# FFN 1's output bias and half of a dot-product sum on GpSimd, and another order of the work on four engines

## The chip, the cores and the metric

The kernel runs on one core of a Trainium2 chip. Five engines run their own instruction streams and meet only at semaphores: TensorE (matmuls into PSUM), VectorE, ScalarE, GpSimd, and SyncE, which here only issues DMAs. The metric is the device time of one execution in microseconds.

## The reference, cut to what matters

The input is 16 images of 96 channels and 96 x 96 pixels; the output has the same shape. Two layers follow each other, each a convolution-like part and a quantized feed-forward network (FFN), with residual sums.

- Layer 0's convolution cuts an image into 3 x 3 patches. In each patch all 9 pixels are scored against 512 vectors (cosine similarity). The best pixel and its best vector are mixed into 96 numbers; with the 9 similarities of that vector they pass a small MLP (leaky ReLU, tanh, ReLU), a linear layer and a 1 x 1 convolution, which gives the patch's 3 x 3 x 96 outputs.
- Each FFN takes a normalized pixel x (96 numbers) and computes `q(W2 q(relu(q(W1 q(x)) + b1))) + b2` with inputs and weights rounded to a float with 2 mantissa bits and sums rounded to 16 bits; the hidden layer has 384 units.
- Layer 1's convolution is a local response normalization (LRN): each pixel is divided by a power of 2 + 1e-4 times a 5 x 5 box sum of squared norms.

## The kernel before, in words

A tile is 128 patches (1152 pixels), and there are 128 tiles, 8 per image. One body is written out for each of 145 steps; each step works on a different tile in each stage, so that all engines always have work. `PARTS` gives the tile of each stage by its offset from the step: `fs` (load, token statistics) is 4 ahead, `f1` (pixel scores) 3, `f2` (window's best vector) 2, `f3` (MLP and conv) 1, `back` (FFN 0's hidden layer) 0, `tail` (its output) -1, `pre`/`rear`/`rtail` (LRN normalization, FFN 1's hidden layer, its output) -11 to -13. The order in which each engine takes the stages' pieces is written out by hand in `body` of that engine; nothing is reordered later, so an instruction that waits holds up all behind it on its engine.

The pieces that the change touches:

- TensorE: `scores(j0, j1)` (L415) are two matmuls per pixel j into one of two PSUM banks, freed by VectorE's maximum. `hidden_units` (L392) and `out_units` (L400) are the FFNs' first and second layer; each FFN has two banks, refilled when ScalarE has copied them. Units 0 to 8 are 3 chunks of 128 hidden units by 3 column groups of 512, 512 and 128; the output is two units of 5 and 4 pixels. `mlp_turn`, `mlp_in`, `mlp_mid`, `mlp_last`, `conv` (L433 to L460) are the MLP, each waiting for a ScalarE step; `win_turn` and `win_scores` (L422, L428) score the chosen pixel.
- ScalarE: `take_hidden` and `take_out` (L552) copy banks to SBUF as f16, `lrn_pixels` (L598) scales x2 into x3, `norm0` and `norm1` (L585) write the FFNs' inputs, `inpT`, `winT`, `h`, `vcs`, `h1` are the MLP's steps.
- VectorE: `score_max` (L824) takes the maximum over 512 scores of a bank. `relu` (L903) adds the bias and applies ReLU to a chunk of 1152 f16 numbers, `round_up` (L911) rounds all 3456 at once. `group_stats` (L815) are per-pixel statistics, `moments`, `pixel_roots` and `select` are chains of small instructions in which each waits for the one before (`run(chain, n)` issues n links), `win_vector` (L864) finds the window's vector. `mlp_input` sums `prod_dot` over channels (L874, 128 x 9 x 96 to 128 x 9), then three scalar products (L875 to L877, once a step), and forms the MLP's input. `residual1` (L894) adds the conv's result to x. `ffn_bias` (L920) adds the FFN's output bias, for FFN 1 and FFN 0 both on VectorE. `lrn_columns`, once an image, is a chain of some 30 links, dealt out between other pieces by `factors`.
- GpSimd: in this order per step, after `root_ready` (the last link of `pixel_roots`, L777): the residual add x2 of FFN 0 (L1080), the gather of the window's vector (an indirect DMA), `keep_root2` (a copy, L1094), `window_parts` once an image, the product `prod_dot` of token tile and vector (L1075), the residual add x4 of FFN 1 (L1080), `tile_columns` (a copy, L1087), the gather of the chosen pixel (L1059).
- SyncE's queue per step: FFN 0's transposes, the store of x4, the loads of the next token tile and of its channel form, FFN 1's transposes.

## Time and profile before

| | us |
|---|---|
| median of 3 runs | 3355.06 (3355.01 to 3362.01) |
| profiled execution, whole | 3366.41 |
| its span in the profile | 3364.6 |
| VectorE busy | 3022.2 (90%) |
| TensorE busy | 2824.8 (84%) |
| ScalarE busy | 2608.5 (78%) |
| GpSimd busy | 1192.6 (35%) |
| mean granted TensorE clock | 0.957 of full speed |

Busy times are shares of the profiled span; an engine's name in the rows is PE (TensorE), PEld (its weight loads), DVE (VectorE), ACT (ScalarE), POOL (GpSimd) or SPq (SyncE's queue). A number such as L911 is the line of the kernel that issued the instruction. The profile's chain of waits that ended last runs over VectorE for 36% of the span, ScalarE 26%, TensorE 25% and DMA 7%.

### The profile page before, as it was taken

What the parts mean: (1) busy time and instruction counts of PE and PEld (TensorE: products, weight loads), DVE (VectorE), ACT (ScalarE), POOL (GpSimd) and SP (SyncE); (2) the same over time, 40 slices, a digit from 0 to 9 for tenths busy, and PEclk for the clock granted to TensorE, in tenths of its full rate; (3) what the DMA queues carried; (4) which work ended last, traced back from release to release, by engine and by line L of the source; (5) the groups of instructions that cost most, each with busy time, mean ns of one, the idle gap of its engine ahead of it and who ended that gap; (6) DMA issues with size and microseconds to landing.
All of it is one profiled execution on the core that took longest, in us unless ns stands there. A gap on an engine that the chain in (4) does not pass through costs nothing.

```text
span 3364.6 us, 55888 instructions
## 1 busy us (share of the span) xinstructions
PE 2824.8 (84%) x15886; PEld 1512.2 (45%) x15886; DVE 3022.2 (90%) x10843; ACT 2608.5 (78%) x7047; POOL 1192.6 (35%) x1159
## 2 busy tenths in 40 slices
PE   5888898988888888888888888888989899889654
PEld 2444444444445444444444444444444445444322
DVE  6888999999999999999999999999999999999532
ACT  0444788888888887878888788888888888888876
POOL 1223243333334333333433433334343434334221
PEclk9999999999999999999999999999999999999755
DMA  3111222222222222232232222223222223232111
GB/s 91 48 55 47 66 69 84 80 72 81 71 73 80 69 83 66 69 82 67 68 84 65 73 79 68 84 68 83 71 82 71 83 70 84 68 84 58 37 48 43
DMA packets 236607, 237.32 MB, mean 71 GB/s; under 512 B 183426, under 2 KB 186764, under 8 KB 236300
## 3 DMA queue, kind: packets, MB, share of 16 engines
q1 hardware_dynamic: 226060, 214.86, 23.2%
q0 software_dynamic: 10240, 18.89, 2.2%
q8 instruction: 129, 2.11, 0.3%
q14 instruction: 178, 1.46, 0.1%
HBM read 134.72 MB, written 57.02 MB: 57 GB/s over the span
## 4 chain that ended last, share of the span: by engine, by line
DVE 36%; ACT 26%; PE 25%; DMA 7%; issue 5%; SPq 0%; POOL 0%; POOLq 0%; DVEq 0%
ACT ffn_hid L552 11%; ACT ffn_x L585 10%; PE banks L415 10%; DVE st L815 7%; DMA ffn_xT<-ffn_x 7%; DVE ffn_hid L911 7%; DVE pix L824 6%; DVE ffn_hid L903 6%; PE banks L392 4%; PE banks L460 4%; PE banks L400 3%; DVE x L894 3%; PE banks L438 2%; ACT h L665 2%; ACT x L598 1%
## 5 line engine op out<-in xcount | busy, mean ns | idle before, releaser
L552 ACT ACTIVATE ffn_hid<-banks 128x512 f16<-128x512 f32 (+1 forms) x2304 | 1052.7, 492 | 387.3 <-PE banks L392 386.6
L415 PE MATMUL banks<-wcT,xc 128*128 128x512 f32 x2304 | 1217.8, 620 | 79.7 <-DVE pix L824 43.6
L392 PE MATMUL banks<-ffn_xT,w1q 128*128 128x512 fp8e5 (+1 forms) x2304 | 706.7, 340 | 260.1 <-ACT ffn_hid L552 170.4
L1080 POOL TENSOR_TENSOR x<-x,ffn_f 128x864 f32<-128x864 f32 x256 | 491.7, 1921 | 1038.5 <-DVE nb L777 920.3
L824 DVE TENSOR_REDUCE pix<-banks 128x1 f32<-128x512 f32 x1152 | 787.1, 684 | 69.0 <-PE banks L415 68.7
L392 PEld LDWEIGHTS banks<-ffn_xT,w1q 128*128 128x128 bf16 x2304 | 219.5, 98 | 783.7 <-ACT ffn_hid L552 541.5
L400 PE MATMUL banks<-w2q,ffn_hid 128*128 128x96 bf16 x6912 | 394.6, 211 | 160.7 <-DVE ffn_hid L911 159.9
L903 DVE TENSOR_SCALAR ffn_hid<-ffn_hid,b1q 128x1152 f16<-128x1152 f16 x768 | 419.3, 559 | 116.0 <-ACT ffn_hid L552 116.0
L400 PEld LDWEIGHTS banks<-w2q,ffn_hid 128*128 128x128 f16 x6912 | 353.1, 101 | 364.1 <-issue 335.0
L598 ACT ACTIVATE x<-x,cols 128x96 f32<-128x96 f32 x1152 | 511.7, 473 | 0.0
L585 ACT ACTIVATE ffn_x<-x,cols 128x96 fp8e5<-128x96 f32 x1152 | 501.4, 485 | 0.0
L415 PEld LDWEIGHTS banks<-wcT,xc 128*128 128x128 f32 x2304 | 392.7, 194 | 209.5 <-DVE pix L824 69.1
L585 ACT ACTIVATE ffn_x<-x,nb,pix 128x96 fp8e5<-128x96 f32 x1152 | 481.2, 469 | 0.0
L815 DVE BATCH_NORM_STATS2 st<-x 128x6 f32<-128x96 f32 x2304 | 424.5, 244 | 19.4 <-POOL x L1080 19.4
L552 ACT ACTIVATE ffn_y<-banks 128x480 f16<-128x480 f32 (+1 forms) x512 | 274.7, 537 | 215.2 <-PE banks L400 215.1
L460 PE MATMUL banks<-wc,h 128*128 128x480 f32 (+1 forms) x1024 | 415.0, 550 | 2.3 <-ACT h L665 2.2
L1075 POOL TENSOR_TENSOR prod_dot<-xt,wrow 128x864 f32<-128x864 f32 x128 | 294.9, 2304 | 164.5 <-DMA wrow<-vector_table,vidx 164.5
L911 DVE TENSOR_SCALAR ffn_hid<-ffn_hid 128x3456 uint16<-128x3456 uint16 x256 | 318.3, 1243 | 4.9
L1059 POOL DMA_INDIRECT win<-x_tok_in,xrow x128 | 142.9, 1117 | 477.4 <-DVE xrow L844 477.4
L460 PEld LDWEIGHTS banks<-wc,h 128*128 128x128 f32 x1024 | 191.8, 195 | 246.4 <-issue 126.8
L1067 POOL DMA_INDIRECT wrow<-vector_table,vidx x128 | 127.0, 992 | 416.1 <-DVE vidx L864 407.7
L815 DVE BATCH_NORM_STATS2 st<-xt 128x6 f32<-128x96 f32 x1152 | 209.8, 244 | 4.8 <-DMA xt<-x_tok_in 4.8
(137 smaller groups left out, 2849.9 us busy)
## 6 DMA issues: line engine op xcount, KB each, us to landing
xt<-x_tok_in SPq DMA_DIRECT2D x128, 432.0 KB
xc<-x_chan_in SPq DMA_DIRECT2D x128, 432.0 KB
out_tok<-x SPq DMA_DIRECT2D x128, 432.0 KB
ffn_xT<-ffn_x SPq DMA_TRANSPOSE x256, 2.6
win<-x_tok_in,xrow POOLq DMA_INDIRECT x128, 3.1
wrow<-vector_table,vidx POOLq DMA_INDIRECT x128, 2.7
shift<-shift_in SPq DMA_DIRECT2D x1, 960.0 KB
vector_table<-wtab SPq DMA_DIRECT2D x1, 384.0 KB, 2.9
```

The source lines that it names most:

```text
L392: last = pe.matmul(bank[:, 0:c1 - c0], w1q[:, ffn.layer, c * P:(c + 1) * P], pairs, start=True, stop=True)
L400: last = pe.matmul(bank[:, (j - j0) * C:(j - j0 + 1) * C], ffn.hid[:, c, j * P:(j + 1) * P], w2q[:, ffn.layer, c, :], start=(c == 0), stop ...
L415: last = pe.matmul(ps_score[score_bank(j)], xc[p][:, j, :], wcT[:, :], start=True, stop=True)
L460: last = pe.matmul(bank[:, 0:(j1 - j0) * C], h1[:, q, :], wc[:, q, j0 * C:j1 * C], start=(q == 0), stop=(q == 1))
L552: return nc.scalar.activation(dst, src, ACT.Copy)
L585: last = nc.scalar.activation(ffn.x8[:, j // 2, 0:C, j % 2], x[:, j, :], ACT.Identity, bias=bias_c[:, j:j + 1], scale=scale_c[:, j:j + 1], ...
L598: last = nc.scalar.activation(x3[:, k.pre3, j, :], x2[:, k.pre & RING - 1][:, j, :], ACT.Identity, bias=cols[k.q][:, 1, j:j + 1], scale=co ...
L815: last = nc.vector.bn_stats(st3[:, which, j, :], src[:, j, :])
L824: nc.vector.tensor_reduce(mx[p][:, j:j + 1], ps_score[score_bank(j)], AX.X, ALU.max).then_inc(score_taken, 1)
L903: nc.vector.tensor_scalar(ffn.hid[:, c, :], ffn.hid[:, c, :], b1q[:, ffn.layer, c:c + 1], 0.0, ALU.add, ALU.max).then_inc(ffn.rounded, 1)
L911: nc.vector.tensor_scalar(bits, bits, TO_E5M2, TO_E5M2, ALU.add, ALU.subtract).then_inc(ffn.hid_ready, 1)
L1080: tt(dst, x, ffn.f[:, :, :], ALU.add).then_inc(ready, 1)
```

## The change

- FFN 1's bias (`ffn_bias(ffn1, ...)`) is taken from VectorE and done on GpSimd, between the gather and `window_parts`.
- After the product `prod_dot` (96 products per pixel) GpSimd adds its two halves into `half_dot` (48 per pixel), after the x4 add; VectorE's sum L874 then reads `half_dot`. A semaphore `dot_chain` orders the two.
- GpSimd's product also waits for `ffn1.hid_ready`, that is for VectorE's `round_up(ffn1)` of the same step.
- GpSimd's copies `keep_root2` and `tile_columns` move to the head of its step, except in the steps with `lrn_columns`, where they stay behind.
- VectorE's step begins with the maximum of score 0; the first three token statistics move into `mlp_input`, the other statistics are split into groups of three; five links of the root chain come in a row; FFN 0's bias comes after the root chain; `relu(ffn1, ...)`, the maxima and `select`/`moments` change places.
- TensorE issues scores 0 and 1 before FFN 0's output units, whose halves now have a score and a hidden unit of FFN 1 between them; the other pieces are moved as shown. ScalarE follows TensorE's order.

```diff
         prod_dot = sb("prod_dot", [P, J, C])
+        half_dot = sb("half_dot", [P, J, C // 2])
         dots = sb("dots", [P, J])
...
-        prod_dot_ready, inp_ready = sem("prod_dot_ready"), sem("inp_ready")
+        dot_chain, prod_dot_ready, inp_ready = sem("dot_pool_chain"), sem("prod_dot_ready"), sem("inp_ready")
...
@@ TensorE, body @@
-        scores(0, 1)
+        scores(0, 2)
         out_units(ffn0, k.tail, k.tail_p, 0)
-        scores(1, 2)
+        scores(2, 3)
+        hidden_units(ffn1, k.rear, 0, 1)
         out_units(ffn0, k.tail, k.tail_p, 1)
-        scores(2, 3)
+        hidden_units(ffn1, k.rear, 1, 2)
         if k.f3 is not None:
             mlp_turn(k.f3)
-        hidden_units(ffn1, k.rear, 0, 2)
+        hidden_units(ffn1, k.rear, 3, 1)
+        if k.f2 is not None:
+            win_turn(k.f2, k.q)
         if k.lrn is not None:
             pe.wait_ge(box_ready, k.lrn + 1)
         if k.f3 is not None:
             mlp_in(k.f3)
-        if k.f2 is not None:
-            win_turn(k.f2, k.q)
-        hidden_units(ffn1, k.rear, 2, 2)
+        hidden_units(ffn1, k.rear, 4, 1)
         scores(3, WIN_TURN)
-        hidden_units(ffn1, k.rear, 4, 1)
         if k.f3 is not None:
             if k.f2 is not None:
                 pe.wait_ge(winT_ready, k.f2 + 1)
             mlp_mid(k.f3)
-        hidden_units(ffn1, k.rear, 5, 2)
+        hidden_units(ffn1, k.rear, 5, 1)
         if k.f2 is not None:
             win_scores(k.f1, k.f2)
+        hidden_units(ffn1, k.rear, 6, 1)
+        scores(WIN_TURN, 5)
+        hidden_units(ffn1, k.rear, 7, 1)
+        scores(5, 6)
         if k.f3 is not None:
             mlp_last(k.f3)
-        hidden_units(ffn1, k.rear, 7, 1)
-        scores(WIN_TURN, 5)
+        scores(6, 7)
         hidden_units(ffn1, k.rear, 8, 1)
-        scores(5, 6)
         if k.f3 is not None:
             conv(k.f3)
-        scores(6, 7)
         hidden_units(ffn0, k.back, 0, 2)
         scores(7, 8)
-        hidden_units(ffn0, k.back, 2, 1)
+        hidden_units(ffn0, k.back, 2, 3)
         scores(8, J)
         window_sums(k, 0, 5)
-        hidden_units(ffn0, k.back, 3, 2)
+        hidden_units(ffn0, k.back, 5, 2)
         out_units(ffn1, k.rear, k.rear_p, 0)
-        hidden_units(ffn0, k.back, 5, 2)
         window_sums(k, 5, 10)
         hidden_units(ffn0, k.back, 7, 2)
...
@@ ScalarE, body @@
-        lrn_pixels(k, 0, 1)
+        lrn_pixels(k, 0, 3)
         take_out(ffn0, k.tail, k.tail_p, 0)
-        lrn_pixels(k, 1, 2)
-        take_out(ffn0, k.tail, k.tail_p, 1)
-        lrn_pixels(k, 2, 3)
+        lrn_pixels(k, 3, 4)
+        take_hidden(ffn1, k.rear, 0, 2)
         if k.f3 is not None:
             act.wait_ge(inp_turned, k.f3 + 1)
             copy(inpT[:, :], ps_a[0:D1, 0:P]).then_inc(inpT_ready, 1)
-        take_hidden(ffn1, k.rear, 0, 2)
+        take_hidden(ffn1, k.rear, 2, 2)
+        take_out(ffn0, k.tail, k.tail_p, 1)
         if k.f2 is not None:
             act.wait_ge(win_turned, k.f2 + 1)
             copy(winT[0:C, :], ps_a[0:C, 0:P]).then_inc(winT_ready, 1)
-        take_hidden(ffn1, k.rear, 2, 1)
         if k.f3 is not None:
             act.wait_ge(z1_made, k.f3 + 1)
             nc.scalar.activation(h[:].rearrange("c m p -> c (m p)"), ps_b[0:C, 0:M1 * P], ACT.Relu,
                                  scale=1.0 - LEAK).then_inc(h_ready, 1)
-        take_hidden(ffn1, k.rear, 3, 1)
-        lrn_pixels(k, 3, 4)
-        norm0(k, 0, 1)
         take_hidden(ffn1, k.rear, 4, 1)
+        norm0(k, 0, 5)
+        take_hidden(ffn1, k.rear, 5, 1)
         if k.f3 is not None:
             act.wait_ge(z2_made, k.f3 + 1)
             nc.scalar.activation(vcs[:, :], ps_a[0:C, 0:P], ACT.Tanh,
                                  bias=bmlp[:, 0:1]).then_inc(vcs_ready, 1)
-        norm0(k, 1, 5)
-        take_hidden(ffn1, k.rear, 5, 1)
-        norm0(k, 5, 6)
+        norm0(k, 5, 7)
         take_hidden(ffn1, k.rear, 6, 1)
-        norm0(k, 6, 7)
+        norm0(k, 7, 8)
         take_hidden(ffn1, k.rear, 7, 1)
         if k.f3 is not None:
             act.wait_ge(z3_made, k.f3 + 1)
@@ -665,24 +662,22 @@
                 last = nc.scalar.activation(h1[0:LH, q, :], ps_b[0:LH, q * P:(q + 1) * P], ACT.Relu,
                                             bias=bmlp[0:LH, 1 + q:2 + q])
             last.then_inc(h1_ready, 1)
+        norm0(k, 8, J)
         take_hidden(ffn1, k.rear, 8, 1)
-        norm0(k, 7, J)
         lrn_pixels(k, 4, XA)
+        norm1(k, 0, 1)
         lrn_pixels(k, XA, 6)
-        norm1(k, 0, 1)
+        norm1(k, 1, 3)
         lrn_pixels(k, 6, 8)
-        norm1(k, 1, 2)
-        take_hidden(ffn0, k.back, 0, 1)
-        norm1(k, 2, 3)
-        take_hidden(ffn0, k.back, 1, 2)
         norm1(k, 3, 4)
+        take_hidden(ffn0, k.back, 0, 2)
         lrn_pixels(k, 8, J)
-        take_hidden(ffn0, k.back, 3, 2)
+        take_hidden(ffn0, k.back, 2, 3)
+        norm1(k, 4, XA)
+        norm1(k, XA, 6)
+        take_hidden(ffn0, k.back, 5, 4)
+        norm1(k, 6, J)
         take_out(ffn1, k.rear, k.rear_p, 0)
-        take_hidden(ffn0, k.back, 5, 1)
-        norm1(k, 4, XA)
-        take_hidden(ffn0, k.back, 6, 3)
-        norm1(k, XA, J)
...
@@ VectorE @@
-        f3c.add(nc.vector.tensor_reduce(dots[:, :], prod_dot[:, :, :], AX.X, ALU.add),
+        f3c.add(nc.vector.tensor_reduce(dots[:, :], half_dot[:, :, :], AX.X, ALU.add),
...
+        def token_stats(j0, j1, between=iter(())):
+            if k.fs is not None:
+                if j0 == 0:
+                    dve.wait_ge(xt_loaded[k.p], landed(k.fs, k.p))
+                return group_stats(1, xt[:, k.fs & XT - 1], j0, j1, between)
+            return last
         run(factors, 1)
+        scores(0, 1)
         if k.f3 is not None:
-            mlp_input(k.f3, k.p, roots_of, lambda: scores(0, 1))
+            mlp_input(k.f3, k.p, roots_of, lambda: token_stats(0, 3))
         else:
-            scores(0, 1)
-        run(roots_of, 1)
-        ffn_bias(ffn1, k.rtail, x4_ready)
-        run(roots_of, 2)
+            token_stats(0, 3)
+        run(roots_of, 5)
         scores(1, 2)
         run(roots_of, 1)
+        scores(2, 3)
+        run(roots_of)
         ffn_bias(ffn0, k.tail, x2_ready)
-        run(roots_of)
-        scores(2, WIN_TURN, factors, 2)
-        if k.fs is not None:
-            dve.wait_ge(xt_loaded[k.p], landed(k.fs, k.p))
-            last = group_stats(1, xt[:, k.fs & XT - 1], 0, 3, factors)
+        run(factors, 1)
+        relu(ffn1, k.rear, 0)
+        scores(3, WIN_TURN, factors, 2)
+        last = token_stats(3, 6, factors)
+        if k.f2 is not None:
+            win_vector(k.f2, k.q, factors)
+        relu(ffn1, k.rear, 1)
+        scores(WIN_TURN, 5, factors, 2)
         if k.tail is not None:
             dve.wait_ge(x2_ready, k.tail + 1)
-            last = group_stats(2, x2[:, k.tail & RING - 1], 0, J, factors)
-        if k.f2 is not None:
-            win_vector(k.f2, k.q, factors)
-        relu(ffn1, k.rear, 0)
-        relu(ffn1, k.rear, 1)
-        scores(WIN_TURN, 5, factors, 2)
+            group_stats(2, x2[:, k.tail & RING - 1], 0, 3, factors)
+        scores(5, 6, factors, 2)
+        if k.tail is not None:
+            group_stats(2, x2[:, k.tail & RING - 1], 3, 6, factors)
+        scores(6, 7, factors, 2)
         relu(ffn1, k.rear, 2)
-        scores(5, 6, factors, 2)
+        run(factors, 1)
         round_up(ffn1, k.rear)
-        if k.fs is not None:
-            last = group_stats(1, xt[:, k.fs & XT - 1], 3, J, factors)
+        last = token_stats(6, J, factors)
+        if k.tail is not None:
+            last = group_stats(2, x2[:, k.tail & RING - 1], 6, J, factors)
         run(factors)
         if k.f3 is not None:
             residual1(k.f3, k.q)
-        scores(6, 7)
-        if k.f3 is not None:
             dve.wait_ge(x1_ready, k.f3 + 1)
             group_stats(0, x1[k.q], 0, 3, iter(()))
         scores(7, 8)
         if k.f3 is not None:
-            group_stats(0, x1[k.q], 3, 6, iter(()))
-        relu(ffn0, k.back, 0)
-        scores(8, J)
-        if k.f3 is not None:
-            last = group_stats(0, x1[k.q], 6, J, iter(()))
+            last = group_stats(0, x1[k.q], 3, J, iter(()))
         if k.stats is not None:
             last.then_inc(stats_ready, 1)
+        scores(8, J)
         select_of = select(k.f1, k.p) if k.f1 is not None else iter(())
         moments_of = moments(k.stats, k.q) if k.stats is not None else iter(())
         for _ in range(3):
+            run(moments_of, 1)
             run(select_of, 1)
-            run(moments_of, 1)
+        relu(ffn0, k.back, 0)
         run(select_of, 1)
+        run(moments_of, 1)
+        run(select_of, 1)
+        run(moments_of, 1)
         relu(ffn0, k.back, 1)
-        for _ in range(4):
-            run(select_of, 1)
-            run(moments_of, 1)
+        run(select_of, 1)
+        relu(ffn0, k.back, 2)
         run(select_of)
         run(moments_of)
-        relu(ffn0, k.back, 2)
         round_up(ffn0, k.back)
...
@@ GpSimd @@
-        tt(prod_dot[:, :, :], xt[:, f2 & XT - 1], unit, ALU.mult).then_inc(prod_dot_ready, 1)
+        tt(prod_dot[:, :, :], xt[:, f2 & XT - 1], unit, ALU.mult).then_inc(dot_chain, 1)
+    def half_product(f2):
+        pool.wait_ge(dot_chain, f2 + 1)
+        tt(half_dot[:, :, :], prod_dot[:, :, 0:C // 2], prod_dot[:, :, C // 2:C],
+           ALU.add).then_inc(prod_dot_ready, 1)
+    def ffn_bias(ffn, tile, added):
+        pool.wait_ge(ffn.taken, (tile + 1) * UNITS + 2)
+        wait_past(pool, added, tile)
+        b2 = b2q[:, ffn.layer, :].rearrange("p (o c) -> p o c", o=1).broadcast_to([P, J, C])
+        tt(ffn.f[:, :, :], ffn.y[:, :, :], b2, ALU.add).then_inc(ffn.f_ready, 1)
...
         if k.moments is not None:
             pool.wait_ge(root_ready, k.moments + 1)
+        if k.root2 is not None and k.lrn is None:
+            keep_root2(k)
+        if k.columns is not None and k.lrn is None:
+            tile_columns(k)
         if k.tail is not None:
             ffn_output(ffn0, k.tail, x1[k.q][:, :, :], x2[:, k.tail & RING - 1], x2_ready)
         if k.f2 is not None:
             gather(k.f2)
-        if k.root2 is not None:
-            keep_root2(k)
+        if k.rtail is not None:
+            ffn_bias(ffn1, k.rtail, x4_ready)
         if k.windows is not None:
             window_parts(k.windows)
         if k.f2 is not None:
+            if k.rear is not None:
+                pool.wait_ge(ffn1.hid_ready, k.rear + 1)
             dot_product(k.f2)
         if k.rtail is not None:
             pool.wait_ge(x4_stored[k.q], landed(k.rtail, k.q))
             ffn_output(ffn1, k.rtail, x3[:, k.rtail3], x4[k.q][:, :, :], x4_ready)
-        if k.columns is not None:
+        if k.f2 is not None:
+            half_product(k.f2)
+        if k.root2 is not None and k.lrn is not None:
+            keep_root2(k)
+        if k.columns is not None and k.lrn is not None:
             tile_columns(k)
         if k.f1 is not None:
             gather_pixel(k.f1, k.p)
```

## Rows read from the trace of the kernel before

**Rows 1.** Busy time by stretch, columns PE PEld DVE ACT POOL (instructions), clock, DMA:

```profile
2783.88:2806.97 23.09, 20.80 (x123) 11.04 (x122) 22.36 (x83) 20.20 (x55) 8.94 (x7) 1.00 0.30 79
...
64.50:3143.30 3078.80, 2680.70 (x15155) 1437.21 (x15156) 2906.66 (x10494) 2438.03 (x6605) 1144.72 (x1098) 0.99 0.27 72
3143.30:3364.60 221.30, 111.56 (x647) 59.15 (x643) 76.98 (x206) 166.48 (x434) 40.65 (x50) 0.53 0.14 42
```

**Rows 2.** Line L875, all and two windows: count, ns min/median/max, first and last start:

```profile
L875 DVE TENSOR_SCALAR mix<-chosen,top x128: 201/204/206, 64.5 to 3143.3; 128x1 f32<-128x1 f32 x128
...
L875 DVE TENSOR_SCALAR mix<-chosen,top x6: 204/205/205, 2691.6 to 2807.0; 128x1 f32<-128x1 f32 x6
...
L875 DVE TENSOR_SCALAR mix<-chosen,top x3: 202/202/206, 2830.5 to 2882.5; 128x1 f32<-128x1 f32 x3
```

**Rows 3.** Costliest groups, the round-up: busy us, mean ns | idle before:

```profile
L911 DVE TENSOR_SCALAR ffn_hid<-ffn_hid 128x3456 uint16<-128x3456 uint16 x256 | 318.3, 1243 | 4.9
```

**Rows 4.** Timelines of GpSimd and VectorE, a longer step: start, us, instruction [idle before]:

```profile
1424.26 2.01 POOL L1075 TENSOR_TENSOR prod_dot<-xt,wrow 128x864 f32<-128x864 f32 x1 [1.56 <-DMA wrow<-vector_table,vidx]
...
1424.40 2.79 DVE L911 TENSOR_SCALAR ffn_hid<-ffn_hid 128x3456 uint16<-128x3456 uint16 x1
```

**Rows 5.** Timelines of VectorE and GpSimd, an ordinary step:

```profile
2795.57 1.05 DVE L911 TENSOR_SCALAR ffn_hid<-ffn_hid 128x3456 uint16<-128x3456 uint16 x1
...
2795.64 2.85 POOL L1075 TENSOR_TENSOR prod_dot<-xt,wrow 128x864 f32<-128x864 f32 x1 [1.50 <-DMA wrow<-vector_table,vidx]
```

**Rows 6.** Timeline of VectorE, head of the ordinary step:

```profile
2782.92 1.05 DVE L874 TENSOR_REDUCE dots<-prod_dot 128x9 f32<-128x864 f32 x1
2783.88 0.20 DVE L875 TENSOR_SCALAR mix<-chosen,top 128x1 f32<-128x1 f32 x1
...
2786.44 0.68 DVE L824 TENSOR_REDUCE pix<-banks 128x1 f32<-128x512 f32 x1
2787.04 0.18 DVE L764 SCALAR_TENSOR_TENSOR pix<-rtmp,pix 128x36 f32<-128x36 f32 x1
2787.14 0.60 DVE L920 TENSOR_TENSOR ffn_f<-ffn_y,b2q 128x864 f16<-128x864 f16 x1
2787.66 0.19 DVE L754 SCALAR_TENSOR_TENSOR rtmp<-pix 128x36 f32<-128x36 f32 x1
```

**Rows 7.** Single lines, all of them: count, ns min/median/max, first and last start:

```profile
L1080 POOL TENSOR_TENSOR x<-x,ffn_f x256: 1807/1821/2651, 113.9 to 3359.9; 128x864 f32<-128x864 f32 x128
...
L1118 POOL TENSOR_TENSOR win<-row x16: 337/342/346, 307.5 to 3209.6; 128x72 f32<-128x72 f32 x16
...
L834 DVE TENSOR_TENSOR sim<-pix x128: 141/151/703, 47.5 to 3114.8; 128x9 f32<-128x9 f32 x128
```

**Rows 8.** Root's end and the x2 add in the ordinary step; line L935:

```profile
2788.35 0.17 DVE L777 SCALAR_TENSOR_TENSOR nb<-pix 128x9 f32<-128x9 f32 x1
...
2788.60 1.82 POOL L1080 TENSOR_TENSOR x<-x,ffn_f 128x864 f32<-128x864 f32 x1 [6.94 <-DVE nb L777]
...
L935 DVE TENSOR_SCALAR lbuf<-lbuf x16: 190/1441/1446, 323.2 to 3222.7; 128x72 f32<-128x72 f32 x16
```

**Rows 9.** Timeline of TensorE, FFN 0's output units after the round-up:

```profile
2806.24 0.80 PE L400 MATMUL banks<-w2q,ffn_hid 128*128 128x96 bf16 x15 [1.03 <-DVE ffn_hid L911]
```

**Rows 10.** Timelines: token load and its first statistics, FFN 1's transposes and first hidden unit:

```profile
2800.75 0.38 SPq L324 DMA_DIRECT2D xt<-x_tok_in  x1
...
2789.71 0.57 DVE L815 BATCH_NORM_STATS2 st<-xt 128x6 f32<-128x96 f32 x3
...
2805.58 1.20 SPq L334 DMA_TRANSPOSE ffn_xT<-ffn_x  x1
...
2786.26 0.59 PE L392 MATMUL banks<-ffn_xT,w1q 128*128 128x512 fp8e5 x2
```

**Rows 11.** Timeline of VectorE, the window's vector and two relus:

```profile
2791.97 0.69 DVE L864 FIND_INDEX8 vidx<-chosen,banks 128x8 uint32<-128x512 f32 x1
2792.57 0.93 DVE L903 TENSOR_SCALAR ffn_hid<-ffn_hid,b1q 128x1152 f16<-128x1152 f16 x2
```

## The prediction

> **What bounds the kernel now.** I read the busy times by stretch first, then the starts of one instruction that occurs once a step, then the costliest groups, then the timelines of VectorE and GpSimd in an ordinary step, in a longer one and in the two steps per image that carry LRN work, last the same step on TensorE and SyncE. The step's clock is L875, the first scalar product of `mlp_input`: 128 of them, 64.5 to 3143.3 us, are 127 intervals with a mean of 24.24 us [rows 2]. In that stretch VectorE is busy for 2906.66 of 3078.8 us (94%), TensorE 2680.70 (87%), ScalarE 2438.03 (79%), GpSimd 1144.72 (37%) [rows 1]. So VectorE sets the pace, with TensorE not far behind.
>
> Not all steps are alike. From 2691.6 to 2807.0 five intervals take 23.08 us each [rows 2]; in one of them VectorE is busy 22.36 of 23.09 us and TensorE 20.80 [rows 1]. The two intervals from 2830.5 to 2882.5 take 52.0 us together [rows 2], 5.8 more than two ordinary ones: the first carries `window_parts`, the second `lrn_columns`. There are 15 such pairs in the 127. Were the other 97 all at 23.08, the sum would be 97 x 23.08 + 15 x 52.0 = 3019 us, 60 under the 3078.8 there are.
>
> Where those 60 us sit: the 256 round-ups of the hidden layer (L911) take 318.3 us together [rows 3], while one alone takes 1.05 [rows 5], so 269 would do: 49 us too many. The two timelines show why. When GpSimd's product `prod_dot` (L1075) begins at 1424.26 and the round-up at 1424.40, the round-up takes 2.79 us, that is until the product is done and then its own time [rows 4]. When the round-up begins at 2795.57 and the product at 2795.64, the product takes 2.85 instead of 2.01 and VectorE loses nothing [rows 5]. The two shut each other out, the first to begin wins, and 0.1 us decides over 1.7 us of VectorE.
>
> **The change part by part.**
>
> *FFN 1's bias to GpSimd.* One f16 add of 864 elements leaves VectorE. L920 starts at 2787.14 and the next instruction at 2787.66: 0.52 us a step [rows 6]. On GpSimd no f16 add with two f16 inputs stands in the trace; its nearest rows are the residual add L1080 with an f16 operand, 1.82 us, and the product with a broadcast operand, 2.01 [rows 4, 7]. I take 1.9 us. GpSimd has room: 8.94 us of 23.09 now [rows 1].
>
> *Half sum on GpSimd.* The reduction L874 over 864 elements takes 0.96 us from start to start (2782.92 to 2783.88), the maximum over 512 takes 0.60 (2786.44 to 2787.04) [rows 6]: 1.02 ns an element, so 432 elements take 0.52. That is 0.44 us a step less on VectorE. The new add of 432 elements on GpSimd lies between 0.34 us (72 elements) and 1.82 (864) [rows 7], in a straight line 1.0 us. GpSimd then has 8.94 + 1.9 + 1.0 = 11.8 us a step, still half empty.
>
> *The product waits for FFN 1's round-up.* The coin toss above is gone: 49 us less, and what stands behind the round-up on GpSimd (product 2.0, x4 add 1.8, half sum 1.0, together 4.8 us) falls on stats, residual and score maxima, none of which a GpSimd add stretches. VectorE has 0.5 + 0.5 + 1.1 + 0.5 + 0.6 + 1.0 + 0.6 = 4.8 us of these and three rounds of `select` and `moments` before its next f16 instruction, `relu(ffn0, 0)`. The cover is just long enough; if it is not, the price is one of the blocks below. The half sum is wanted only in the next step.
>
> *The new order at the step's head.* The wait ahead of FFN 0's second layer (TensorE idle 1.03 us until the round-up is done [rows 9]) is filled: two scores now stand before it. VectorE begins with a maximum and the first three token stats, and the root chain, whose links wait for one another, is done before FFN 0's bias instead of around it. The links had both biases and a maximum between them; five in a row now cost about 0.04 us of idle each, 0.2 a step at most. ScalarE takes the second half of FFN 0's output after four hidden units of FFN 1: from the round-up's end I count 4.9 us on ScalarE, and the bias that needs it comes at 5.5. It fits by half a microsecond.
>
> *Moved past SyncE's queue.* The token stats of the newly loaded tile move from 2789.71 to the head, about 5.4 us earlier in the step. Their load is issued at 2800.75 of the step before [rows 10], so 6 us are left of 12; no wait for it exists now, and I put it at nothing, at most 0.3. FFN 1's transposes start at 2805.58 and TensorE's first hidden unit used to come at 2786.26, 3.8 us after the same point a step earlier [rows 10]; now it comes before `mlp_turn`, some 1.3 us sooner. Some of the wait for that transfer returns, 0 to 0.3 us on TensorE, which has 1.3 us of slack. Zero to 0.1 on the step.
>
> *What becomes late next.* FFN 0's add (x2, 1.82 us) used to begin when the root was ready (2788.60 [rows 8]) and lie under maxima and stats. Now it begins after FFN 0's bias and two small copies, about 0.9 us behind the bias, and ends 2.7 behind it. VectorE does after the bias one relu (0.46), a maximum (0.60), three stats (0.49) and `win_vector` (0.66) [rows 6, 10, 11], then `relu(ffn1, 1)`: 2.2 us behind. By rows 4 it waits for the add: 0.5 us. If `win_vector` itself is late by that much, the block costs nothing; if the copies go first, `relu(ffn1, 0)` waits 0.2 as well. Between 0 and 0.7; I take 0.3, since TensorE reaches the window's score with about 0.1 us to spare by my count of its work.
>
> A rule of the Trainium skill bears on this place (SBUF — State Buffer, "Who interferes with whom"): VectorE and GpSimd share one pair of ports as an exclusive lock held for a whole instruction, and even a VectorE `tensor_tensor` with two SBUF inputs takes part against a GpSimd instruction that reads SBUF. The first half agrees with rows 4 and 5. The second speaks against the change, which puts FFN 0's bias beside GpSimd's copies; the one case at hand is L834, 0.15 us in the median and 0.70 at most [rows 7]. By that rule the step would be up to 0.2 us longer, 20 us in all.
>
> Sum of an ordinary step: 23.08 - 0.52 - 0.44 = 22.12; + 0.3 for the blocked relu, + 0.1 for transfers and hand-overs: 22.5 us. VectorE's work in it would be 21.4 us and TensorE's still 20.8, so there is little below this.
>
> *The two LRN steps.* `window_parts` (some 5 us of small GpSimd instructions) still stands before the product and now also behind the bias, so product, x4 add and half sum run 4 to 5 us later than in an ordinary step, into FFN 0's relus. One block of up to 1.8 us more, or the product waits as now: +0.6 for the step, between 0 and 1.8. In the `lrn_columns` step L935 takes 1.44 us in the median, since it begins inside the x2 add, and 0.19 at the least [rows 8]. In the new order it begins just before that add, and `relu(ffn1, 0)` is the one that may be caught instead: I leave it, between 1.25 less and 0.5 more. The pair then costs 5.8 + 0.6 = 6.4 above two ordinary steps: 51.4 us.
>
> Sum: 97 x 22.5 + 15 x 51.4 = 2953.5 us, 125 under 3078.8. The end (3143.3 to 3364.6) has VectorE at 77 of 221 us and TensorE at half its clock (0.53 granted) [rows 1]; only FFN steps are left, paced by ScalarE and the hand-overs. The longer bias is on its last chain once, +1.3; the new order may give or take 5. I put it at nothing. Span 3364.6 - 125 = 3239; the profiled execution took 1.8 us more than its span (3366.4), so 3241. The median of the runs, 3355.1, lies 11 below the profiled one, about six blocked round-ups; as the new kernel has no coin toss, I take nothing off.
>
> **The rivals.**
>
> *All covers hold.* VectorE loses only what is removed: steps of 22.1 us and pairs of 44.2 + 5.8 - 1.25 = 48.8, 2876 us for the 127, 203 less: 3163. For it: steps of 23.08 repeat to 0.01 us now, so the engines lock into a rhythm. Against it: TensorE would be at 94% with hand-overs inside.
>
> *TensorE and ScalarE become the bound.* TensorE's 20.8 us of work and its waits for bank exchanges make 23.0 us of the ordinary step and 52.4 of a pair: 3017 us, 62 less: 3305. For it: now it already waits about 1 us in several small pieces besides the 1.03 that goes. Against it: its work is not made longer, and the scores lie more evenly between the hidden units.
>
> *GpSimd catches a relu in every step (the other side).* FFN 0's add begins just before `relu(ffn1, 0)` or the x4 add or half sum just before `relu(ffn0, 0)`, and VectorE stands still for 1.8 us as in rows 4, but each time: 22.1 + 1.8 = 23.9 us and pairs of 54.2, 3131 us, 52 more: 3419. It decides from 1.6 us of blocks in the ordinary step. For it: two more GpSimd instructions and an add moved next to a relu. Against it: the relu starts 0.08 us before the bias ends (as 2787.66 stands to 2787.14 + 0.60 [rows 6]), GpSimd 0.08 after its releaser (2788.60 to 2788.35 + 0.17 [rows 8]).
>
> **How the numbers follow.** Forecast 50%, all covers 18%, TensorE and ScalarE 20%, caught in every step 12% (of it 3 for a mild form that ends level). The likeliest is 3241. The range goes nearly to the first rival below and a little beyond the second above: 3165 to 3325. About 0.2% is what a measurement can tell from no change: faster 0.88, within it 0.03, slower 0.09.
>
> **What would show it.** The distance of the once-a-step instruction: 22.5 us if right, 22.1, 23.0 or 23.9 for the rivals. L911 at 1.05 us in all 256. L903 above 0.6 us in the mean would show relus caught by GpSimd, and which of the five positions. VectorE's busy share stays at 94% or more if it is still the bound; if it falls under 92%, TensorE's waits for ScalarE or ScalarE's for TensorE have grown. L824 waiting for L415, L894 for L460 or L920 for L552 would each show a cover that was too short. The forecast is wrong if the ordinary step stays above 23 us without a blocked relu, or if the end grows by more than 10 us.

## The result, and the profile after it

The changed kernel takes 3322.34 us in the median of 4 runs (3318.05 to 3325.16), beside 3355.72 for the kernel before on the same chip: a ratio of 0.9889, 95% interval 0.9876 to 0.9903. That is faster by 33 us, 1.1%, and clear of the spread of the runs. The forecast was 114 us less (3241); the time lies just inside the upper end of the range, 3325. The direction was right, the size was not.

The page of the changed kernel, engines and chain; the last two lines are the chain's shares by engine and by line:

```profile
span 3323.4 us, 56026 instructions
...
PE 2793.8 (84%) x15886; PEld 1506.5 (45%) x15886; DVE 2927.0 (88%) x10715; ACT 2646.0 (80%) x7047; POOL 1516.7 (46%) x1415
...
PE 39%; ACT 21%; DVE 20%; DMA 13%; issue 5%; POOL 1%; SPq 0%; POOLq 0%; ACTq 0%; DVEq 0%
PE banks L416 13%; DMA ffn_xT<-ffn_x 12%; ACT ffn_hid L553 9%; PE banks L393 8%; ACT ffn_x L586 7%; PE banks L401 4%; DVE st L810 4%; ACT x L599 4%; PE banks L429 3%; DVE ffn_hid L898 3%; DVE pix L819 3%; PE banks L439 2%; PE banks L447 2%;
```

VectorE fell from 90% to 88% of the whole span. The prediction's 94% and 92% were meant for the stretch of the 127 steps; there VectorE went from 94% to 92.5% (2814.89 of 3042.15 us, below), so its sign of another bound was just not reached. But VectorE's share of the chain fell from 36% to 20%. The FFNs' transposes (`ffn_xT<-ffn_x`) alone are 12% of the chain, where all DMAs together had been 7%.

Stretches of the changed kernel, to be read beside [rows 1]: a fast ordinary step, a slow ordinary step, all 127 steps from the first L870 (the L875 of before) to the last, and the end:

```profile
1715.40:1737.54 22.14, 20.26 (x121) 10.99 (x121) 21.30 (x82) 20.50 (x56) 11.36 (x9) 1.00 0.28 83
2292.70:2316.34 23.64, 20.43 (x121) 10.93 (x120) 21.41 (x82) 20.51 (x56) 11.08 (x9) 1.00 0.33 76
63.97:3106.12 3042.15, 2650.67 (x15144) 1431.40 (x15143) 2814.89 (x10380) 2474.40 (x6605) 1438.73 (x1338) 0.98 0.29 73
3106.12:3323.40 217.28, 110.86 (x658) 59.41 (x654) 71.96 (x191) 167.68 (x435) 69.60 (x65) 0.54 0.14 43
```

The 127 steps take 3042.15 us where 3078.80 stood and 2953.5 was forecast. Sorted by kind from the starts of L870, the 97 ordinary ones (the first 8 counted with them) take 22.99 us in the mean (forecast 22.5), a pair with `window_parts` and `lrn_columns` 25.97 + 28.16 = 54.1 (forecast 51.4). The first excess is 0.49 x 97 = 47 us, the second 2.73 x 15 = 41, together the 88 that are missing. VectorE does 21.3 to 21.4 us of work in a fast and a slow step alike, as predicted (21.4), and TensorE 20.3 to 20.4; what the slow step has more, 1.5 us, are waits.

Groups and waits of the changed kernel: the round-up, the two new GpSimd operations and the relu (busy us, mean ns | idle before), then three waits (us in total, times, longest):

```profile
L898 DVE TENSOR_SCALAR ffn_hid<-ffn_hid,b1q 128x1152 f16<-128x1152 f16 x768 | 411.5, 536 | 111.2 <-ACT ffn_hid L553 111.2
...
L906 DVE TENSOR_SCALAR ffn_hid<-ffn_hid 128x3456 uint16<-128x3456 uint16 x256 | 273.0, 1067 | 8.3
...
L1091 POOL TENSOR_TENSOR ffn_f<-ffn_y,b2q 128x864 f16<-128x864 f16 x128 | 234.8, 1835 | 38.6 <-ACT ffn_y L553 36.9
...
L1083 POOL TENSOR_TENSOR half_dot<-prod_dot 128x432 f32<-128x432 f32 x128 | 141.1, 1103 | 1.2
```

```profile
PE banks L401 <- DVE ffn_hid L906: 226.2, 148, 5.7
...
PE banks L393 <- DMA ffn_xT<-ffn_x: 109.0, 102, 3.8
...
DVE vidx L859 <- PE banks L429: 67.3, 112, 2.1
```

The coin toss is gone: 273.0 us of round-ups instead of 318.3 [rows 3]; one of the 256, behind the last step, is still held (2.56 us). The two new GpSimd operations cost what was estimated (1.84 us for 1.9, 1.10 for 1.0), and the relu's mean of 0.54 us says that GpSimd hardly ever catches one. But TensorE now waits 102 times for the FFNs' transposes (76.8 us in 70 waits before). Counted apart by where in the step they fall, those for FFN 1's, within the 127 steps, are 69 waits and 60.7 us, where they had been 45 and 24.5. And VectorE waits 112 times for TensorE's scores of the window, where it had waited 4 times, 2.5 us in all.

### The profile page after: what moved, and what is told of

Read it like the earlier page. It is cut to its first block, busy times and chain, and to the rows that moved or that the text cites. A ratio compares the mean times of both kernels' runs of the same rounds, so it can differ in the third digit from the quotient of the medians.

```text
span 3323.4 us, 56026 instructions
## 1 busy us (share of the span) xinstructions
PE 2793.8 (84%) x15886; PEld 1506.5 (45%) x15886; DVE 2927.0 (88%) x10715; ACT 2646.0 (80%) x7047; POOL 1516.7 (46%) x1415
## 4 chain that ended last, share of the span: by engine, by line
PE 39%; ACT 21%; DVE 20%; DMA 13%; issue 5%; POOL 1%; SPq 0%; POOLq 0%; ACTq 0%; DVEq 0%
PE banks L416 13%; DMA ffn_xT<-ffn_x 12%; ACT ffn_hid L553 9%; PE banks L393 8%; ACT ffn_x L586 7%; PE banks L401 4%; DVE st L810 4%; ACT x L599 4%; PE banks L429 3%; DVE ffn_hid L898 3%; DVE pix L819 3%; PE banks L439 2%; PE banks L447 2%; PE banks L461 2%; DVE ffn_hid L906 2%
## 5 line engine op out<-in xcount | busy, mean ns | idle before, releaser
L393 PE MATMUL banks<-ffn_xT,w1q 128*128 128x512 fp8e5 (+1 forms) x2304 | 727.1, 341 | 205.4 <-DMA ffn_xT<-ffn_x 109.0
L416 PEld LDWEIGHTS banks<-wcT,xc 128*128 128x128 f32 x2304 | 408.4, 193 | 264.1 <-issue 191.8
L599 ACT ACTIVATE x<-x,cols 128x96 f32<-128x96 f32 x1152 | 488.0, 459 | 19.1 <-POOL cols L1103 19.1
L586 ACT ACTIVATE ffn_x<-x,cols 128x96 fp8e5<-128x96 f32 x1152 | 475.9, 460 | 4.2
L553 ACT ACTIVATE ffn_y<-banks 128x480 f16<-128x480 f32 (+1 forms) x512 | 255.6, 526 | 214.3 <-PE banks L401 214.3
L1110 POOL COPY img<-pix 128x27 f32<-128x27 f32 x128 | 39.3, 307 | 772.0 <-DVE nb L772 770.2
L1078 POOL TENSOR_TENSOR prod_dot<-xt,wrow 128x864 f32<-128x864 f32 x128 | 258.2, 2018 | 265.4 <-DVE ffn_hid L906 241.7
L906 DVE TENSOR_SCALAR ffn_hid<-ffn_hid 128x3456 uint16<-128x3456 uint16 x256 | 273.0, 1067 | 8.3
L1091 POOL TENSOR_TENSOR ffn_f<-ffn_y,b2q 128x864 f16<-128x864 f16 x128 | 234.8, 1835 | 38.6 <-ACT ffn_y L553 36.9
L1062 POOL DMA_INDIRECT win<-x_tok_in,xrow x128 | 127.3, 994 | 259.6 <-DVE xrow L839 259.6
```

Of the source, the lines that this page charges most:

```text
L393: last = pe.matmul(bank[:, 0:c1 - c0], w1q[:, ffn.layer, c * P:(c + 1) * P], pairs, start=True, stop=True)
L416: last = pe.matmul(ps_score[score_bank(j)], xc[p][:, j, :], wcT[:, :], start=True, stop=True)
L553: return nc.scalar.activation(dst, src, ACT.Copy)
L586: last = nc.scalar.activation(ffn.x8[:, j // 2, 0:C, j % 2], x[:, j, :], ACT.Identity, bias=bias_c[:, j:j + 1], scale=scale_c[:, j:j + 1], ...
L599: last = nc.scalar.activation(x3[:, k.pre3, j, :], x2[:, k.pre & RING - 1][:, j, :], ACT.Identity, bias=cols[k.q][:, 1, j:j + 1], scale=co ...
L906: nc.vector.tensor_scalar(bits, bits, TO_E5M2, TO_E5M2, ALU.add, ALU.subtract).then_inc(ffn.hid_ready, 1)
```

## Experiments

All times are medians beside the kernel before on the same chip (3355 to 3361 us). In the kernels made from the changed one, the numbers of lines are up to 5 higher. "Ordinary step" stands from here on for the 89 without the first 8, where not all stages have work yet.

**FFN 1's transposes and the loads.** What makes a slow ordinary step slow stands on TensorE at its head. The fast step and the slow one of the changed kernel, TensorE:

```profile
1715.15 1.09 PE L416 MATMUL banks<-wcT,xc 128*128 128x512 f32 x2
1716.08 0.38 PE L393 MATMUL banks<-ffn_xT,w1q 128*128 128x512 fp8e5 x1
...
2292.43 1.09 PE L416 MATMUL banks<-wcT,xc 128*128 128x512 f32 x2
2294.85 0.38 PE L393 MATMUL banks<-ffn_xT,w1q 128*128 128x512 fp8e5 x1 [1.33 <-DMA ffn_xT<-ffn_x]
```

and SyncE's queue ahead of each, issues only:

```profile
1710.02 0.55 SPq L318 DMA_DIRECT2D xc<-x_chan_in  x1
1712.75 1.20 SPq L335 DMA_TRANSPOSE ffn_xT<-ffn_x  x1
...
2287.66 0.59 SPq L318 DMA_DIRECT2D xc<-x_chan_in  x1
2289.80 1.20 SPq L335 DMA_TRANSPOSE ffn_xT<-ffn_x  x1
```

In the slow step the transposes are issued 2.1 us after the load of `xc` and land 4.9 us after their issue; in the fast one it is 2.7 and 3.0. TensorE then starts FFN 1's hidden units 2.15 us after the step's start instead of 0.68, and the rest of the step is 1.5 us late. So the first theory: the transposes stand behind the load's packets in SyncE's queue, and moving them ahead gives a step of 22.1 us. Two ways of moving them, and the same in the kernel before as a control:

```diff
 # a_xc_last; b_xc_last likewise from the kernel before
-load(Step(k.k + 1))
+load_tokens(nxt.fs, nxt.p)
 turn(ffn1, k.pre)
+load_pixels(nxt.fs, nxt.p)
 # a_xt_first: load_tokens, store of x4, turn(ffn1), load_pixels
```

> The changed kernel, with one edit: SyncE issues the load of the channel tile (xc, wanted two steps later) after FFN 1's transposes instead of before them. Theory T (transfers): in the changed kernel the transposes are issued 2.2 us behind that load (4.4 before the change), end 3.7 us after their issue in the median instead of 2.1, and are wanted 1.5 us sooner; TensorE's first hidden unit of FFN 1 waits for them, and that wait sets the step. Then the transposes end about 2.1 us after issue, the ordinary step falls from a mean of 23.1 to 22.1 to 22.4 us, and the time by 60 to 85 us, to about 3245 us. Rival R (TensorE and ScalarE are the bound and the transfer is only where the wait shows): the wait moves to another line, the time falls by 15 us at most, and stays over 3305.

> The changed kernel, with SyncE's queue in the order FFN 0's transposes, token load, store of x4, FFN 1's transposes, channel load. The token load no longer waits behind x4. T: as for the run with only the channel load moved, within 5 us of it (3240 to 3250), a little better in the LRN pairs, where x4 is late and the two loads and the store are bunched ahead of the transposes. R: no fall beyond 15 us, as there.

> The kernel before, with the channel load issued after FFN 1's transposes. T: before the change the transposes had 1.6 us to spare in the ordinary step, so nothing or up to 10 us less: 3345 to 3356. If the old kernel, too, were held by this transfer (rival), it would lose 30 us or more.

Measured: 3256.38 (ratio 0.9693, 0.9676 to 0.9711), 3251.28 (0.9676, 0.9659 to 0.9693) and 3370.95 (1.0024, 1.0006 to 1.0042). Theory T holds. The ordinary step's median falls from 23.04 to 22.15 us in both. Landing of the transposes after their issue (min/median/max) in the kernel before, in the changed kernel and in a_xt_first, and then TensorE's wait for them in a_xt_first (102 times, 109.0 us in the changed kernel):

```profile
DMA to landing us min/median/max: 2.6/2.6/5.9
```

```profile
DMA to landing us min/median/max: 2.4/2.9/6.5
```

```profile
DMA to landing us min/median/max: 2.4/2.6/4.5
```

```profile
PE banks L397 <- DMA ffn_xT<-ffn_x: 51.6, 38, 3.8
```

These rows mix both FFNs. From the packets, FFN 1's alone ended 2.12 us after their issue in the median before, 3.73 (up to 5.58) in the changed kernel and 2.24 in a_xt_first. TensorE's waits for them within the 127 steps fall from 60.7 us to 1.9, in 4 waits; what is left of the 51.6 us belongs to FFN 0 and to the two ends of the run. The kernel before gains nothing from the same edit (11 us more in the median, 0.2%): there the transposes were issued 4.4 us after the load in the median, not 2.2, and ended on time. So the queue's order costs the changed kernel 71 us, and it is the change that made it matter: the change lets TensorE want the transposes 1.3 us sooner and leaves the load just ahead of them.

**The coin toss alone.** The kernel before, with nothing but the product's wait for FFN 1's round-up:

```diff
+pool.wait_ge(ffn1.hid_ready, k.rear + 1)
 dot_product(k.f2)
```

> The kernel before, with one edit: GpSimd's product waits for FFN 1's round-up, as in the changed kernel. Theory C (the product and the round-up shut each other out, and this costs the old kernel 49 us): all 256 round-ups take 1.05 us, ordinary steps stay at 23.1, the time falls by 40 to 55 us to about 3308. Rival: the later product pushes the x4 add into FFN 0's relu or makes the MLP input late, and the gain is under 20 us.

Measured: 3320.24 (0.9891, 0.9871 to 0.9911), 40 us (by the ratio 37) less, at the low end of the expected 40 to 55, with all 256 round-ups at 1.04 to 1.08 us. One line gives as much as the whole change. The counterpart, the new kernel (with a_xt_first's queue) without that wait:

> Same base (3251 us); GpSimd's product no longer waits for FFN 1's round-up. Theory C: the product is ready to start about 0.7 us before the round-up in every ordinary step, so the round-up waits for it: L911's counterpart takes 2.3 to 2.5 us each time, the ordinary step 23.4 to 23.6, the time +100 to +170 us. Rival: the wait is worth only what it was worth in the old order, where 44 of 128 collided: +40 to +50 us.

Measured: 3694.99 (1.1005, 1.0975 to 1.1034), ordinary steps of 26.5 us in the mean. That is 444 us more than a_xt_first, where 100 to 170 were expected. VectorE and GpSimd in one of the steps:

```profile
2322.47 2.13 DVE L902 TENSOR_SCALAR ffn_hid<-ffn_hid,b1q 128x1152 f16<-128x1152 f16 x1
2324.63 2.56 DVE L910 TENSOR_SCALAR ffn_hid<-ffn_hid 128x3456 uint16<-128x3456 uint16 x1
```

```profile
2320.47 1.84 POOL L1095 TENSOR_TENSOR ffn_f<-ffn_y,b2q 128x864 f16<-128x864 f16 x1
2322.25 2.02 POOL L1082 TENSOR_TENSOR prod_dot<-xt,wrow 128x864 f32<-128x864 f32 x1
2324.22 2.05 POOL L1100 TENSOR_TENSOR x<-x,ffn_f 128x864 f32<-128x864 f32 x1
```

Three GpSimd instructions follow each other without a gap; the relu is held until the product is done and ends 0.33 us after it, then the round-up is held by the x4 add and ends 0.92 us after it. Not every step is like this one: 65 round-ups of 256 take over 1.2 us (1 in a_xt_first) and 83 relus of 768 over 0.7 (7). The loss has a second part, which no run separates from the first: within the 127 steps TensorE runs 447 us at the lower of its two clock levels, for 85 in a_xt_first. Either way the new order hangs on the wait.

**The bias of FFN 1.** The prediction had booked it as 0.52 us off each step. If VectorE's work set the pace, putting it back would cost that:

```diff
+ffn_bias(ffn1, k.rtail, x4_ready)   # VectorE, and gone from GpSimd
 ffn_bias(ffn0, k.tail, x2_ready)
```

> The changed kernel with SyncE's queue as in the run that moved both loads (3251 us), and FFN 1's bias back on VectorE, just ahead of FFN 0's. Theory V (with the transfer out of the way VectorE sets the step, so each instruction of its own costs what it takes): 0.52 us more in each of 127 steps, +60 to +70 us, about 3315, ordinary step 22.7. Rival R (TensorE and ScalarE hold the step at 22.1): +20 us at most.

> The changed kernel with only FFN 1's bias back on VectorE; SyncE's queue as in the changed kernel. Theory H: the bias hides ahead of win_vector here too, and the LRN pairs lose 3.5 us less each, as with the other queue: 3322 falls by 35 to 60 us, to about 3272, while the ordinary step stays near 23. Theory V of the prediction (VectorE's 0.52 us a step count): +66 us, 3388.

Measured: with a_xt_first's queue 3199.21 (0.9514, 0.9498 to 0.953), 52 us *less* than with the bias on GpSimd, which neither theory had; with the changed kernel's own queue 3274.56 (0.9745, 0.9716 to 0.9774), 48 less, as was then expected. In ordinary steps it makes no difference (median 22.15 both ways with a_xt_first's queue). Why nothing is lost shows at the window's index, VectorE in an ordinary step of a_xt_first, then of a_bias_dve (where "x2" are both biases):

```profile
1907.07 0.60 DVE L919 TENSOR_TENSOR ffn_f<-ffn_y,b2q 128x864 f16<-128x864 f16 x1
1909.62 0.09 DVE L863 MATCH_VALUE_LOAD vidx<-chosen,banks 128x8 f32 x1 [0.43 <-PE banks L433]
```

```profile
1903.89 1.13 DVE L919 TENSOR_TENSOR ffn_f<-ffn_y,b2q 128x864 f16<-128x864 f16 x2
1906.45 0.08 DVE L863 MATCH_VALUE_LOAD vidx<-chosen,banks 128x8 f32 x1
```

VectorE stood idle 0.43 us before L863, waiting for TensorE's window scores; the bias fills that hole. Why something is gained shows in the pair. VectorE and GpSimd in the changed kernel's pair that begins at 2191.43:

```profile
2209.28 1.86 DVE L790 TENSOR_TENSOR mtmp<-st 128x27 f32<-128x27 f32 x1
2211.06 1.09 DVE L829 TENSOR_TENSOR sim<-pix 128x9 f32<-128x9 f32 x1
...
2227.49 2.24 DVE L942 TENSOR_SCALAR cols_i<-lbuf 128x72 f32<-128x72 f32 x1
```

```profile
2200.15 1.83 POOL L1091 TENSOR_TENSOR ffn_f<-ffn_y,b2q 128x864 f16<-128x864 f16 x1
...
2209.25 1.83 POOL L1096 TENSOR_TENSOR x<-x,ffn_f 128x864 f32<-128x864 f32 x1
2211.03 1.10 POOL L1083 TENSOR_TENSOR half_dot<-prod_dot 128x432 f32<-128x432 f32 x1
...
2227.82 1.83 POOL L1091 TENSOR_TENSOR ffn_f<-ffn_y,b2q 128x864 f16<-128x864 f16 x1
```

In the window step the bias stands ahead of `window_parts`, so the x4 add and half sum come 1.8 us later, into `moments` and `select`: L790, 0.20 us alone, ends when the x4 add ends, and L829, 0.16 alone, when the half sum ends. In the LRN step L942 ends 0.08 us after the bias. L790, L829 and L942 do this in 14 of the 16 images. With the bias on VectorE (a_xt_first's queue) the pair takes 23.74 + 26.29 us, not 25.29 + 27.68, which is 44 of the 52 us; another 5 lie in the end; and L942 takes 0.32. The same bias kept on GpSimd, but put first in its step, just behind FFN 0's round-up:

> Same base (3251 us); GpSimd does FFN 1's bias first in its step, after VectorE's round-up of FFN 0 of the step before, instead of between gather and window_parts. Theory B (GpSimd's adds and VectorE's two-input and f16 instructions shut each other out, and what the LRN pairs lose, they lose to these): L942's counterpart, which takes 2.2 us because the bias runs, falls to 0.2, and in the window step product, x4 add and half sum run 1.8 us earlier and block moments and select less: 2 us and 1 to 2 us per image, -40 to -60 us, about 3200; ordinary steps stay at 22.1. Rival: at the step's head the bias blocks the MLP input's chain instead (1.8 us on the path), and the time rises by 50 us or more.

Measured: 3197.14 (0.9507, 0.9491 to 0.9523): level with VectorE's version. It was not the engine but the place in GpSimd's queue that cost 50 us.

**Work without order, order without work.** b_work is the kernel before with both adds on GpSimd and the wait, in the old order. a_order is the new order with a_xt_first's queue, the bias and the whole 864-element sum on VectorE:

> The kernel before with the work moved and no reordering: FFN 1's bias and the half sum on GpSimd, product after the round-up; the order on TensorE, ScalarE and VectorE and SyncE's queue as before. Theory V: VectorE loses 0.97 us a step and nothing takes its place: ordinary step 22.1 to 22.5, 3200 to 3250 us, so the new order as such cost time. Rival O: the old order has TensorE's wait of 1.03 us ahead of FFN 0's output and its 20.8 us of work, and cannot follow: ordinary step over 22.7, time over 3275, so the new order was needed.

> The new order alone: the changed kernel with SyncE's queue as in the run that moved both loads, FFN 1's bias and the whole 864-element sum back on VectorE (no half sum). Theory H (the step is held by a chain: VectorE without a gap from win_vector to FFN 0's round-up, then TensorE and ScalarE from FFN 0's output to the window's score; VectorE's work ahead of win_vector hides behind the latter): the sum stands ahead of win_vector, where VectorE now waits 0.16 us for the score, but it also feeds mlp_turn, on which TensorE's chain hangs; so 0.2 to 0.44 us a step, +25 to +55 us over the 3199 of the run with the bias on VectorE: 3225 to 3255. Rival: the sum is hidden like the bias, +10 us at most. Rival V (every VectorE instruction counts): +56 us.

Measured: 3461.38 (1.0299, 1.0282 to 1.0317), worse than either theory had it, and 3213.36 (0.9566, 0.954 to 0.9592). In b_work, two of VectorE's relus in one step (alone 0.51 us):

```profile
1943.53 1.86 DVE L905 TENSOR_SCALAR ffn_hid<-ffn_hid,b1q 128x1152 f16<-128x1152 f16 x1
...
1961.66 1.47 DVE L905 TENSOR_SCALAR ffn_hid<-ffn_hid,b1q 128x1152 f16<-128x1152 f16 x1 [0.34 <-ACT ffn_hid L554]
```

The x4 add (1943.25 to 1945.06) holds `relu(ffn0, 0)` and the bias (1960.98 to 1962.79) holds `relu(ffn1, 2)`: each relu ends a third of a microsecond after the add, and 342 relus of 768 take over 0.7 us, for 128 in b_dot_waits. Beside b_dot_waits, which has the same wait and none of the work moved, the work moved in the old order costs 141 us.

The other run says more. a_order moves none of the work, and still takes 107 us less than b_dot_waits; its ordinary step is 22.35 us in the median, for 23.09 there. One of them (columns as in [rows 1]; its timeline shows no wait on VectorE):

```profile
1471.82:1494.17 22.35, 20.78 (x121) 10.91 (x120) 22.04 (x83) 20.60 (x57) 8.81 (x7) 1.00 0.28 83
```

So it is the order that shortens the step, down to VectorE's own work. The half sum then takes VectorE out of the way, and the step goes to 22.15 us, where a_bias_dve (VectorE busy 21.73) and a_xt_first (21.31) both stand: that is the chain over TensorE and ScalarE. a_order is 14 us above a_bias_dve (by the ratios 17, on another chip), so the half sum is worth 14 to 17 us, 0.1 to 0.2 a step and not 0.44. The expected 25 to 55 was too much.

**Two last versions.** The x4 add of the window step, moved behind FFN 0's round-up, should also spare `select` and `moments`:

```diff
-if k.rtail is not None:                          # GpSimd, behind the product
+if k.rtail is not None and k.windows is None:
     ffn_output(ffn1, k.rtail, ..., x4_ready)
 ...
+if k.rtail is not None and k.windows is not None:   # last in the step
+    wait_past(pool, ffn0.hid_ready, min(k.k + 1, NT))
+    ...
+    ffn_output(ffn1, k.rtail, ..., x4_ready)
```

Both kernels are a_bias_dve with this edit, SyncE's queue being `load_tokens`, `turn(ffn1)`, store, `load_pixels`. a_best also takes the factor chain's links away from score maximum 3 and from token stats 3 to 5; a_best2 leaves them.

> The run with the bias on VectorE (3199 us), with three edits against the blocks of the LRN pair: in the window step GpSimd does the x4 add last, behind FFN 0's round-up, so that moments and select don't meet it; SyncE issues FFN 1's transposes before the store of x4; in the lrn_columns step the first links of the factor chain no longer stand beside the x2 add. Theory B: window step 23.9 to about 22.4, lrn step 26.3 to about 25.2, ordinary unchanged at 22.15: -30 to -45 us, about 3160. Rival: the links are only shifted and TensorE's idle in the lrn step stays, -10 us at most.

> The changed kernel with FFN 1's bias back on VectorE just ahead of FFN 0's, FFN 1's transposes ahead of the loads of the next tiles in SyncE's queue, and, in the 16 window steps alone, the x4 add moved behind FFN 0's round-up. It differs from the version that took 3230 us in one thing: the links of the factor chain stay between the score maxima 3 to 6. My reading of that version is that its LRN steps grew from 26.3 to 29.1 us because the factors' last links came late, and that its window steps fell from 23.7 to 23.3. If that reading holds: ordinary steps 22.45, window steps 23.3, LRN steps 26.3, so about 3190 us, 5 to 10 below the best so far (3197 to 3199). Rival: the late x4 add itself makes the LRN steps long (the next step's window sums or transposes wait for x4): then LRN steps stay near 29 us and the time near 3230.

Measured: 3230.09 (0.961, 0.9585 to 0.9635), a miss (some 3160 was expected), and 3194.21 (0.951, 0.9495 to 0.9526), near the expected 3190. The window step fell to 23.3 us in a_best and 23.4 in a_best2. a_best's LRN step grew to 29.1, for 26.4 in a_best2, because the factor chain's last links came after the round-up, beside the product, the x4 add and the half sum:

```profile
2187.17 1.88 DVE L753 SCALAR_TENSOR_TENSOR lbuf<-cols_i 128x72 f32<-128x72 f32 x1
2189.14 1.69 DVE L756 TENSOR_TENSOR lbuf<-lbuf 128x72 f32<-128x72 f32 x1
2190.93 0.96 DVE L763 SCALAR_TENSOR_TENSOR cols_i<-lbuf,cols_i 128x72 f32<-128x72 f32 x1
```

a_best2 has the lowest median of all, 163 us under the kernel before beside it, and by the two ratios (0.951, 0.9889) some 127 under the changed one. But by the ratios it cannot be told from a_bias_head (0.9507) and a_bias_dve (0.9514): that moving the x4 add pays is not shown.

## Why the prediction was wrong, step by step

**Right.** *The product's wait* (49 us forecast): 37 to 40 measured alone, round-ups all at 1.06. *GpSimd's durations*: 1.84 and 1.10 us for 1.9 and 1.0. *Relus*: the rival of a relu caught in every step fell, and of the 0.3 us a step allowed for a blocked one under 0.1 came. *The end*: 217.3 us for 221.3.

**Right by luck: the bare sum of the ordinary step, 22.12.** The fast steps of the changed kernel take 22.14, and 22.15 is the median once the transposes are on time. But the sum was 23.08 less 0.52 for the bias and 0.44 for the half sum. Measured, the bias gave nothing there and the half sum 0.1 to 0.2. The rest, 0.74 (23.09 to 22.35), came from the new order, which had no gain of its own in the sum.

**Wrong, the first step: "Moved past SyncE's queue ... Zero to 0.1 on the step."** I had noted that FFN 1's hidden units come 1.3 us sooner, and set against it 1.3 us of slack on TensorE. Both halves failed. The transposes do not land at a fixed distance: with the load's packets just ahead they took 3.7 us in the median and up to 5.6, for 2.1. And there was no slack: from the round-up of FFN 0 over its output, FFN 1's hidden units, the MLP and the window's scores to L859 the step is one chain through TensorE and ScalarE, so what is late at its head is late at the window's index (67.3 us of waits there, for 2.5). It measured 71 us (3322 to 3251), 75 with the bias on VectorE (3275 to 3199), where 0 to 13 had been allowed. That alone is most of the 81 us between the forecast and the result; the errors below are as large or larger, but point both ways and nearly cancel.

**Wrong, the second: "FFN 1's bias to GpSimd ... 0.52 us a step."** The instruction did leave VectorE, but the step did not get shorter by it, since VectorE would have waited for the window's scores instead: 0 in the ordinary step. And in the pairs it cost, the term "+0.6 for the step, between 0 and 1.8" for the window step and nothing for the LRN step. Together the bias is +48 to +52 us where the prediction had it at -66 (0.52 x 127). I had looked for blocks at relus and round-ups only. The blocked instructions are tiny f32 ones, 0.2 us alone and up to 1.87 held. The rule quoted in the prediction (the Trainium skill, SBUF — State Buffer, "Who interferes with whom") says just this of a `tensor_tensor` with two SBUF inputs. The traces of L790 and L829 agree with the rule, and I gave it 20 us. [rows 8] had another tiny instruction that was held, the 1.44 us of L935, a `TENSOR_SCALAR` with one input like L942, and I took it as the LRN step's peculiarity.

**Wrong, the third: "*The new order at the step's head*" has costs and no gain.** I weighed whether the pieces would fit and booked nothing for what they give. a_order against b_dot_waits has it at 107 us (by the ratios 109) with the transposes on time.

**Wrong in size: the half sum**, 0.1 to 0.2 us a step for 0.44, 14 to 17 us for 56.

The runs make a path from the one kernel to the other: 3357 before; 3320 with the wait; 3213 with the new order and the transposes ahead of the load (a_order); 3199 with the half sum (a_bias_dve); 3251 with the bias on GpSimd (a_xt_first); 3322 with the load ahead of the transposes. That it ends at the changed kernel is so by construction, and the gains would be split otherwise along another path; the second step changes two things, of which the queue's order gave nothing in the old order (b_xc_last). The rival "TensorE and ScalarE become the bound" (3305) came nearest, and for a reason that it named only in part: their chain does set the step, but what it lost was lost to a DMA, not to bank exchanges.

Open: why the transposes come late by amounts that differ from step to step. The first packet comes 1.19 to 3.3 us after the issue. The distance from the load is part of it, but in the 61 steps where that is 2.1 to 2.2 us the last packet still ends anywhere from 2.7 to 4.9 us after the issue. No run separated packets queued on one of the 16 DMA engines from the queue's own order.

## What to carry over

Before counting an instruction off the busiest engine as gained, look at what that engine waits for next after it is gone, and follow that wait back: here the new order and the half sum brought VectorE level with a chain over TensorE and ScalarE, and the removed 0.5 us turned into 0.4 us of waiting. And give a new order a term of its own: here it was worth more than all the work moved. When work moves earlier, list every DMA that it reads, and what stands ahead of that DMA in its queue. And place every GpSimd add against *all* VectorE instructions with SBUF inputs, the 0.2 us ones too: this bias was free in 97 steps and cost about 1.5 us in each of the other 30.
